# Where the degree products stand in a four-layer graph kernel: second half into the third layer, one addition moved ahead of the sums' copy

## The reference, cut to what matters

```
x = x + relu((adj @ h) @ W.T + b)                                  # layer 0
att = adj * sigmoid((2 + 2 qm @ k.T) / att_scale + att_bias)       # layer 1
support = att @ h ;  x = x + support / norm(support)
deg = max(adj.sum(axis=1), 1e-8) ;  w = adj / deg                  # layer 2
agg_i = sum_j w_ij * logmap(x_i, x_j) ;  x = x + expmap0(agg @ weight + bias)
x = x + w(rank of the non-zeros of adj in their row) @ (h @ weight)  + bias   # layer 3
```

## Time and profile before

| what | value |
|---|---|
| median of 3 runs | 1046.24 us (1044.83 to 1047.54) |
| the profiled execution's own time | 1039.64 us |
| its span, first to last instruction | 1037.9 us |
| PE busy | 981.5 us (95%) |
| DVE busy | 855.9 us (82%) |
| ACT busy | 754.0 us (73%) |
| POOL busy | 229.9 us (22%) |
| mean granted clock of PE | 0.983 of 2.4 GHz |

### The profile page before, as it was taken

The page is one execution under the profiler, slowest core; times in us unless marked ns, Lnnn a source line. Parts: engine busy times, 40 slices in busy tenths (PEclk is TensorE's granted clock), DMA queues, the critical chain, the costliest instruction groups (busy, mean ns, idle before and its releaser), DMA issues.

```text
span 1037.9 us, 16360 instructions
## 1 busy us (share of the span) xinstructions
PE 981.5 (95%) x6147; PEld 468.0 (45%) x6147; DVE 855.9 (82%) x1108; ACT 754.0 (73%) x800; POOL 229.9 (22%) x140
## 2 busy tenths in 40 slices
PE   6999999998999999999979988999999999999898
PEld 2443444544544444335534443444554454434455
DVE  6999999896677768999669986878788977897882
ACT  4555556574667666786698999988888888996683
POOL 1061000000000000023025374443433434441001
PEclk9999999999899999999989999999999999998999
DMA  9989999984278787788644345455545553446562
GB/s 321 421 314 422 410 402 341 321 316 193 91 241 293 242 302 276 262 281 271 221 158 162 123 141 183 163 178 187 170 158 175 188 164 121 142 140 200 199 213 83
DMA packets 96349, 238.43 MB, mean 230 GB/s; under 512 B 16400, under 2 KB 45072, under 8 KB 79888
## 3 DMA queue, kind: packets, MB, share of 16 engines
q1 hardware_dynamic: 87056, 220.62, 61.6%
q10 hardware_dynamic: 9216, 16.78, 4.2%
HBM read 219.55 MB, written 17.83 MB: 229 GB/s over the span
## 4 chain that ended last, share of the span: by engine, by line
PE 65%; DVE 17%; ACT 8%; issue 6%; DMA 2%; SPq 1%; POOL 1%; DVEq 0%; ACTq 0%; POOLq 0%
PE PS L592 43%; PE PS L791 7%; PE PS L925 4%; PE PS L894 4%; DVE work L1839 3%; DVE work L2172 2%; ACT work L1326 2%; ACT work L1334 2%; DVE work L2160 2%; DVE ring L2178 1%; ACT work L1337 1%; DVE work L2166 1%; DVE TB L1619 1%; PE PS L604 1%; PE PS L625 1%
## 5 line engine op out<-in xcount | busy, mean ns | idle before, releaser
L1235 ACT ACTIVATE work<-PS,att_sc 128x1024 f32<-128x1024 f32 x128 | 149.3, 1202 | 77.4 <-PE PS L791 56.2
L1839 DVE TENSOR_TENSOR work<-work,ring 128x1024 f32<-128x1024 f32 x128 | 153.4, 1230 | 50.0 <-ACT work L1235 50.0
L592 PE MATMUL PS<-ring,work 128*65 128x256 f32 (+1 forms) x600 | 190.9, 466 | 3.8 <-DVE work L2199 3.8
L570 POOL TENSOR_TENSOR ring<-work,ring 128x1024 f32<-128x1024 f32 x57 | 135.3, 2375 | 233.1 <-DVE work L2172 233.0
L1148 ACT ACTIVATE work<-PS 128x1024 uint8<-128x1024 f32 x128 | 124.2, 1024 | 85.1 <-PE PS L592 84.8
L2166 DVE SCALAR_TENSOR_TENSOR work<-PS,work 128x1024 f32<-128x1024 f32 x72 | 88.0, 1223 | 55.0 <-PE PS L592 46.5
L592 PEld LDWEIGHTS PS<-ring,work 128*65 128x65 f32 x600 | 80.6, 138 | 90.7 <-issue 65.5
L1326 ACT ACTIVATE work<-work 128x1024 f32<-128x1024 f32 x72 | 76.0, 1055 | 34.8 <-DVE work L2160 34.7
L592 PE MATMUL PS<-work 128*64 128x512 f32 (+2 forms) x544 | 90.9, 484 | 2.5 <-DVE work L1839 1.2
L2172 DVE SCALAR_TENSOR_TENSOR work<-work 128x1024 f32<-128x1024 f32 x72 | 87.9, 1220 | 2.7 <-ACT work L1341 2.1
L894 PE MATMUL PS<-TB,TA 64*128 64x512 f32 x288 | 81.3, 641 | 2.9 <-DVE work L2166 2.9
(11 more groups left out here) (304 smaller groups left out, 1483.9 us busy)
## 6 DMA issues: line engine op xcount, KB each, us to landing
ring<-in_adj_t SPq DMA_DIRECT2D x96, 1024.0 KB, 6.1
ring<-in_adj_t SPq DMA_DIRECT2D x104, 512.0 KB, 4.1
work<-in_adj_t SPq DMA_DIRECT2D x32, 1024.0 KB, 8.7
codes<-work ACTq DMA_DIRECT2D x64, 256.0 KB, 7.3
ring<-codes SPq DMA_DIRECT2D x64, 256.0 KB, 4.3
H<-in_adj_t SPq DMA_DIRECT2D x24, 512.0 KB, 4.1
X<-in_x SPq DMA_DIRECT2D x2, 256.0 KB, 5.4
X<-in_x SPq DMA_DIRECT2D x1, 512.0 KB, 11.0
```

Source lines behind the costliest of these rows:

```text
L570: nc.gpsimd.tensor_tensor(near(n), sums(n), near(n), ALU.mult).then_inc(sem("near_ready"), 1)
L592: return mm(out_ap, lhsT, rhs, start=starts, stop=True, skip_group_check=True)
L1235: nc.scalar.activation(att[:, u, :], PS[:, (4 + 2 * u) * BANK:(6 + 2 * u) * BANK], ACT.Sigmoid, bias=att_sc[:, 2:3], scale=att_sc[:, 1:2]) ...
L1839: V.tensor_tensor(prob[:, m % 4, :], att[:, u, :], ring[:, s % RING, u * UNIT:(u + 1) * UNIT], ALU.mult)\
```

## The change

Four parts. (1) `LATER` names tile 1 in place of tile 2: in layer 0 the addition of step 61 is made and that of step 62 left out, and layer 1 adds in step 33 and no more in step 34. The one-column copies go to columns of their own. (2) Half 0's 16 products are split into 4 ahead of the wait for the sums' copy, 4 behind `to_nodes`, 8 behind `fold_both`, and the waits for the codes and the additions stand ahead of them all; the `keep_at_work` are 8, not 4. (3) Half 1's 16 products leave steps 61 and 62 of layer 1 and stand in layer 2 behind units 1 (4 products), 2 (8) and 3 (4), in bank 3. (4) The clamp of half 1 goes from the end of layer 1 to the head of DVE's unit 4, and the first far gather waits for it.

```diff
--- before.py
+++ after.py
@@ -35,7 +35,7 @@
 MADE = 8
 
 
-LATER = (0, 2, 5, 12, 18, 21, 24)
+LATER = (0, 1, 5, 12, 18, 21, 24)
 
 
 def later_than(s):
@@ -731,13 +731,15 @@
                     ins = mm(PS[:, bank * BANK + t:bank * BANK + t + 1], TB[:, t * P:(t + 1) * P], ones[:, :], start=True, stop=True)
                 return ins
 
+            pe.wait_ge(sem("codes_made"), 4 * T)
+            pe.wait_ge(sem("deg_added"), T)
+            degrees(range(TG // 4), 7)
             pe.wait_ge(sem("sums_out0_v"), 1)
             to_nodes(wbd["l0"][:, :], UNIT, 2, 0).then_inc(sem("z0_ready"), 1)
+            degrees(range(TG // 4, TG // 2), 7)
             fold_both(0)
-            pe.wait_ge(sem("codes_made"), 4 * T)
-            pe.wait_ge(sem("deg_added"), T)
-            degrees(range(TG), 7).then_inc(sem("deg_summed"), 1)
-            for _ in range(4):
+            degrees(range(TG // 2, TG), 7).then_inc(sem("deg_summed"), 1)
+            for _ in range(8):
                 keep_at_work(6)
             pe.wait_ge(sem("khl_out"), 1)
 
@@ -840,12 +842,6 @@
                 if o == 27:
                     pe.wait_ge(sem("aux_r_out_a"), 1)
                     turn_left(0, 0)
-                if o == 29:
-                    pe.wait_ge(sem("aux_l_out"), 1)
-                    pe.wait_ge(sem("deg_late"), 2 * len(LATER))
-                    degrees(range(TG, TG + TG // 2), 0)
-                if o == 30:
-                    degrees(range(TG + TG // 2, T), 0).then_inc(sem("deg_summed"), 1)
 
             for s in range(2 * T):
                 scores(s, 0)
@@ -999,6 +995,8 @@
             def gather2_far(n):
                 S, p = UNITS[n]
                 pe.wait_ge(sem("far_ready"), mirrors(n))
+                if mirrors(n) == 1:
+                    pe.wait_ge(sem("deg_out"), 2)
                 if mirrors(n) > 1:
                     pe.wait_ge(sem("far_out"), mirrors(n) - 1)
                 if n >= AUX_L and mirrors(n) == mirrors(AUX_L - 1) + 1:
@@ -1030,7 +1028,6 @@
                     sides2(n)
                 if n == 1:
                     pe.wait_ge(sem("sums_out1"), 2)
-                    pe.wait_ge(sem("deg_out"), 2)
                     to_nodes(ident[:, :], 2 * UNIT, 0).then_inc(sem("support_ready"), 1)
                 if 1 <= n <= NU and mirrored(n - 1):
                     mirror2(n - 1)
@@ -1042,6 +1039,13 @@
                     second_half2(FLIPS.index(n))
                 second_aux2(n)
                 last_passage2(n)
+                if n == 1:
+                    pe.wait_ge(sem("deg_late"), 2 * len(LATER))
+                    degrees(range(TG, TG + TG // 4), 3)
+                if n == 2:
+                    degrees(range(TG + TG // 4, TG + 3 * TG // 4), 3)
+                if n == 3:
+                    degrees(range(TG + 3 * TG // 4, T), 3).then_inc(sem("deg_summed"), 1)
             gather2_near(NU - 2)
             pe.wait_ge(sem("sum_ready"), NU)
 
@@ -1613,7 +1617,8 @@
             def degree0(h, s, k):
 
                 if isinstance(s, int) and 2 * T - 1 - s in LATER:
-                    V.tensor_copy(trest[:, 0:1], ones[:, :]).then_inc(sem("deg_added"), 1)
+                    k = LATER.index(2 * T - 1 - s)
+                    V.tensor_copy(trest[:, k:k + 1], ones[:, :]).then_inc(sem("deg_added"), 1)
                 elif not isinstance(s, int) or s not in (0, T):
                     dve.wait_ge(sem("deg_added"), s)
                     V.tensor_tensor(TB[:, h * HALF:(h + 1) * HALF], TB[:, h * HALF:(h + 1) * HALF], ring0(k), ALU.add)\
@@ -1948,9 +1953,6 @@
                 product(s, 1)
                 if s - T in LATER:
                     degree1(s, 1)
-                if s == 2 * T - 1:
-                    dve.wait_ge(sem("deg_summed"), 2)
-                    V.tensor_scalar(deg[:, TG:T], PS[:, TG:T], 1e-8, None, ALU.max).then_inc(sem("deg_out"), 1)
                 if s >= T:
                     first_half1(s - T)
 
@@ -2201,6 +2203,9 @@
             EARLY = (17, NU - 3)
             rest2(0)
             for n in range(NU):
+                if n == 4:
+                    dve.wait_ge(sem("deg_summed"), 2)
+                    V.tensor_scalar(deg[:, TG:T], PS[:, 3 * BANK + TG:3 * BANK + T], 1e-8, None, ALU.max).then_inc(sem("deg_out"), 1)
                 if n >= 3 and mirrored(n - 3):
                     far2_out(n - 3)
                 if n >= 3 and closes(n - 3) and n - 3 not in EARLY:
```

## The result

The changed kernel takes 1040.06 us (median of 22 runs, 1032.35 to 1045.72) where the kernel before takes 1046.28 (22 runs, 1036.82 to 1048.34): a ratio of 0.9942, 95% interval 0.9927 to 0.9958, or some 6.1 us less (4.4 to 7.6). The forecast was 1041.9 us, 4.4 less. The profiled execution of the changed kernel took 1037.51 us over a span of 1035.8, only 2.1 us less than that of before. How a gap of 2.1 and one of 6.1 go together is the first thing to read.

The account below looks back on a forecast made before the run. The chain of waits lay on PE for 65% of the span, so PE was taken as the bound. -3.76 + 0.41 + 0.79 - 1.82 = -4.38 us gave 1041.9 us; range with 8 chances in 10: 1039.2 to 1046.0 us.

Parts of the forecast that it names:

- Layer 1's end: Steps 61 and 62 of layer 1: two groups of 8 degree products leave PE's chain, -3.76 us.
- Ahead of the sums' copy: End of layer 0: step 61's addition covers DVE's wait for ACT's root, so the copy comes earlier, -0.81 us.
- Steps 33 and 34: Layer 1: an addition between step 33's two DVE products stalls PE's gather, +0.79 us.
- Layer 2's first units: Moved products fit PE's gaps behind units 1 and 2; behind unit 3 they delay DVE's unit 4 sum, +0.41 us.
- From layer 0 to layer 1: Four products enter PE's wait, four more fills cost time, first scores return to full clock: -1.82 us with the earlier copy.
- rival A: Between layers 0 and 1 the clock comes back fully: -3.95 us there, 1039.7 us in all; chance 0.14.
- rival E: From 252 to 275 us PE's clock falls and stays at half into layer 1: 1048.8 us; chance 0.10.
- From the profile to the median: Whole kernel: the 6.6 us between the profiled execution and the runs' median carried over unchanged, giving 1041.9 us.
- The sum of -4.4: Whole kernel: the forecast's terms added up, -4.38 us, from 1046.24 to 1041.9 us; chance 0.50.

Follow-up runs that it names:

- e9: Changed kernel with the biases cut on ACT and DVE, not POOL, and tile 1's two additions in layer 1's step 34, not 33: 1035.92 us.
- e13: Kernel before with parts 1 and 2 of the change alone and the biases cut on ACT and DVE, not POOL: 1038.59 us.
- e7: Changed kernel with the cutting of the biases moved from POOL to ACT and DVE: 1035.51 us.
- e7b: The kernel of e7 (changed, biases off POOL) run once more, on another chip: 1034.45 us.
- e2: Kernel before with parts 1 and 2 of the change alone: 1043.61 us, ratio 0.9972.
- e11: Changed kernel with the biases off POOL and 15 of half 1's 16 degree products left out: 1035.03 us.
- e12: Changed kernel with the biases off POOL and four fills before the first scores, not eight: 1036.15 us.
- e8: Kernel before with the cutting of the biases moved from POOL to ACT and DVE: 1039.81 us.
- e16: e9 with nine fills in PE's wait for the sums' copy and the four degree products from there put behind the turn to nodes: 1031.80 us.
- e15: e9 with four fills added behind the first four degree products, in PE's wait for the sums' copy: 1033.18 us.
- e1: Kernel before with parts 3 and 4 of the change alone: 1041.13 us against 1046.85, ratio 0.9949.

## Why the prediction was right, step by step

- **Layer 1's end, -3.76: right.** 111.7 to 107.7, -3.98 in every kernel with the products moved. What was late next was PE itself.
- **Ahead of the sums' copy, -0.81: right**, -0.91 (4.30 to 3.39).
- **Steps 33 and 34, +0.79: right**, +0.89, and e9 shows that it is the backlog of two neighbouring steps.
- **Layer 2's first units, +0.41: slightly too high.** The wait for the sides is there (0.90 us), and unit 4's sum starts 0.17 us later than before. The second mirror is not held by it: it starts ahead of that sum (549.05 against 549.26). Unit 4's mirror, which waits for DVE behind it, comes 34.35 us after the first scores, where it came 34.32 after in before and 34.12 in e13, which also has these products in layer 1. So 0.2 us at most shows here, in single executions.
- **From layer 0 to layer 1, -1.82: no single number.** The forecast priced the fills as what brings the clock back. The profile after shows -3.73, rival A's figure nearly, with DVE's chain last; there eight fills at half clock were followed by scores at full clock, as forecast. Other executions of the same passage, against the same 19.71 us, show -1.6 (e7) and -2.1 (e7b), and +1.8 (e2), which is rival E. The step that does not hold is that twice the fills bring the clock back: in e2, e9 and e11 the scores behind eight fills still start at half clock, and e12, with four, has a fall as long and is 0.8 us shorter. In these four the fall begins 0.8 to 1.3 us ahead of the turn to nodes and lasts 17 us; in e7, e7b and e13, with the same work up to there, it begins with the turn or at most 0.3 us behind its start and is over before the turn ends. So what matters lies ahead of the fills; what it is, no run shows. The Trainium skill, page "TensorE: Matmul & The Clock Gate", section "HAM oscillation — how this bites in real kernels", spoke for E: it says that bursts separated by waits have the clock fall again each time. The trace of e2 agrees as to the fall, which comes at 253.1 in PE's wait for the copy; the profile after shows that it need not come there. Why it lasts 17 us in e2, with PE occupied, is open.
- **From the profile to the median: the hole.** 6.6 us between the profiled execution and the median of before were carried over unexplained. They are the cast (7.0 us by e8). Since most executions of both kernels have it, the difference held; the prediction did not know that, so this step was luck.

The sum of -4.4 came out at -6.1 (4.4 to 7.6) in the usual executions and at -4.3 without the cast. What makes the difference of 1.8 us is open: the last column of the table moves by up to 3.3 us with the clock, and no run shows that the edits cause it. The terms of layers 1 and 2 are right by their mechanism; that the total came so near owes something to luck, since the passage between the layers alone can give -3.7 or +1.8.

## What to carry to other kernels

Before a profile is taken as typical, its own time is to be set beside the median; a gap as large as the change can have one cause, and that may be worth more than the change (here 7.0 us against 6.1). Work of a few us on the busiest engine moves well to where that engine waits for another, and then costs next to nothing; an addition moved by one step can cost most of its length (0.89 us here) if the step beside it has one too. Fills behind the wait did not pay: where the clock had fallen, eight cost 0.8 us more than four. Inside the wait nine of them kept the clock up into the turn in one execution (e16), four did not (e15); the medians do not settle what that is worth.

## What the hardware did that was not expected

A POOL cast of 128 x 384 elements took 7.04 us in one execution, 8.26 in e2's and 86.6 and 87.0 us in those of after and of e1. It ends when DVE, busy with additions and comparisons over SBUF, first pauses, be it for 0.34 us. In e2 that is a gap of 0.70 us, in e1 DVE's stop at the end of its additions; first e2's lines, then e1's:

```profile
60.61 8.26 POOL L508 CAST bcut<-bias 128x384 bf16<-128x384 f32 x1
...
66.22 2.28 DVE L1622 TENSOR_TENSOR TB<-TB,work 128x2048 f32<-128x2048 f32 x1
```

```profile
60.82 86.97 POOL L508 CAST bcut<-bias 128x384 bf16<-128x384 f32 x1
...
145.15 2.28 DVE L1621 TENSOR_TENSOR TB<-TB,work 128x2048 f32<-128x2048 f32 x1
```

In all four executions the cast ends 0.36 or 0.37 us after the end of the DVE instruction ahead of the pause. The Trainium skill, page "SBUF — State Buffer", section "Who interferes with whom", says that DVE and POOL share a pair of ports and that the second to issue is blocked until the first instruction has finished. The trace agrees that POOL is held up, but for far longer than an instruction: over 80 us of DVE instructions one behind the other, of which none lasts over 2.3 us.
